# A 2752-byte gap in SBUF ahead of the turned rows of the expert products

## What is computed

```
x = layernorm(x + linear_attention(x))          # 16 heads, five 512x512 weights
x = layernorm(x + cross_attention(x, ctx))      # softmax over 512 positions, 16 heads
x = layernorm(x + experts(x))                   # 16 experts, the best 4 of each token
# the experts, in short:
top_val, top_idx = top_k(x @ router.T + b, 4);  w = softmax(top_val)
gate, up = x @ Wg[e] + bg[e], x @ Wu[e] + bu[e]
gate = min(gate, 7); up = clip(up, -7, 7)
y_e  = ((up + 1) * gate * sigmoid(1.702 * gate)) @ Wd[e] + bd[e]
out  = sum over the 4 experts of w_e * y_e
```

## Time and profile before

| | us |
|---|---|
| median of three runs | 1549.84 |
| runs | 1543.59 to 1550.4 |
| span of the profiled execution, first to last instruction | 1545.7 |
| steady part of the experts, gate of tile 2 to gate of tile 75 | 676.96 |
| one tile of it | 9.27 |

### The profile page before, as it was taken

How to read it: one execution, slowest core, us unless ns; L and a number is a source line. 1 busy time by engine, 2 the same in 40 slices (tenths; PEclk the granted TensorE clock), 3 DMA queues, 4 the chain that set the end, 5 groups by cost and what they waited for, 6 DMA issues and landing times. The chain is left out here.

```text
span 1545.7 us, 27131 instructions
## 1 busy us (share of the span) xinstructions
PE 1438.5 (93%) x7546; PEld 1024.1 (66%) x7546; DVE 953.9 (62%) x1426; ACT 730.2 (47%) x1416; POOL 866.9 (56%) x706
## 2 busy tenths in 40 slices
PE   6999999799999999998959999999999999999990
PEld 5878888434444444443547888888888888888870
DVE  2334343877888778888855555555555555555554
ACT  4212221178787787775433444434344443444233
POOL 4435332555677658644556646656666676476222
PEclk9999999989999999997869999999999999999995
DMA  5201003555485585651175546656666566473336
GB/s 202 85 22 51 14 32 66 84 97 70 88 148 117 89 147 115 92 109 47 56 242 140 152 99 168 169 115 174 153 161 159 156 165 164 118 196 81 64 58 231
DMA packets 93630, 181.36 MB, mean 117 GB/s; under 512 B 19097, under 2 KB 21913, under 8 KB 92473
## 3 DMA queue, kind: packets, MB, share of 16 engines
q1 hardware_dynamic: 73800, 133.04, 34.1%
q0 software_dynamic: 18544, 46.13, 14.9%
q10 hardware_dynamic: 1152, 0.52, 0.2%
HBM read 116.32 MB, written 33.73 MB: 97 GB/s over the span
## 5 line engine op out<-in xcount | busy, mean ns | idle before, releaser
L952 DVE TENSOR_REDUCE stage<-ps_a 128x2 f32<-128x1024 f32 x256 | 300.2, 1218 | 74.5 <-PE ps_a L1301 73.8
L750 ACT ACTIVATE probs<-ps_b 128x512 f32<-128x512 f32 x504 | 274.2, 596 | 52.2 <-PE ps_b L1316 47.7
L2086 POOL TENSOR_TENSOR we_split<-we_raw,we_split 128x512 f32 (+1 forms) x192 | 248.6, 1532 | 84.0 <-ACT we_split L2077 82.1
L2408 PE MATMUL ps_y<-we_split,hT 128*128 x912 | 231.5, 402 | 2.9 <-DVE hT L2330 2.9
L2408 PE MATMUL ps_u<-we_split,xT 128*128 x912 | 230.9, 402 | 0.0
L2408 PE MATMUL ps_g<-we_split,xT 128*128 x912 | 227.0, 397 | 0.5 <-POOL we_split L2086 0.5
L2408 PEld LDWEIGHTS ps_g<-we_split,xT 128*128 128x128 f32 x912 | 172.0, 189 | 42.9 <-issue 0.9
L2408 PEld LDWEIGHTS ps_y<-we_split,hT 128*128 128x128 f32 x912 | 165.5, 188 | 38.1 <-issue 3.3
L2408 PEld LDWEIGHTS ps_u<-we_split,xT 128*128 128x128 f32 x912 | 166.2, 189 | 34.1
L2250 ACT ACTIVATE hT<-ps_h 128x512 fp32r<-128x512 f32 x76 | 45.2, 595 | 303.2 <-PE ps_h L2380 263.4
L2198 POOL DMA_INDIRECT scratch_acc<-x_keep,to_rows x76 | 121.2, 1594 | 109.3 <-issue 49.9
(11 more groups left out here) (345 smaller groups left out, 2208.9 us busy)
## 6 DMA issues: line engine op xcount, KB each, us to landing
we_raw<-in_w_expert SPq DMA_DIRECT2D x180, 256.0 KB
stack<-xT_raw SPq DMA_DIRECT2D x192, 128.0 KB, 5.5
we_bias<-in_b_expert SPq DMA_DIRECT2D x16, 768.0 KB, 4.4
stage<-in_w SPq DMA_DIRECT2D x5, 1024.0 KB, 5.4
xT_raw<-in_xT SPq DMA_DIRECT2D x4, 1024.0 KB, 6.8
x_tok<-in_x POOLq DMA_DIRECT2D x16, 256.0 KB, 3.0
acc_sb<-scratch_acc SPq DMA_DIRECT2D x8, 512.0 KB, 8.0
out<-res_sb SPq DMA_DIRECT2D x8, 512.0 KB, 4.6
```

The lines of the kernel that those rows point to most:

```text
L750: nc.scalar.activation(probs[:, n % 3, h], src[:], ACT.Exp, scale=DH ** -0.5).then_inc(b_kept, 1)
L952: nc.vector.tensor_reduce(out[:, :, i, k % NC], ps_a[i][:], AX.X, ALU.max, negate=True).then_inc(a_kept[i], 1)
L2086: nc.gpsimd.tensor_tensor(lo, W["raw"][:, k, c], hi, ALU.subtract).then_inc(W["lo"], 1)
L2408: mm = nc.tensor.matmul(out[:], left[:, a, c], w[:, bass.ds(par, 1), k, b, c].squeeze(1), start=(n == 0), stop=(n == len(passes) - 1))
```

## The change

One buffer is allocated and never used. It stands between `row_weight` and `xT4`, and has 688 float32 per partition, 2752 bytes. No instruction is added, removed or reordered.

More of the change, by code:

```diff
@@ L2107, in experts @@
         weight = sb("row_weight", [P, U, 2])
+        sb("beside_rows", [P, 688])
         xT = sb("xT4", [P, 2, 2, KC, P], F32R)
```

## The result

With the gap the kernel takes 1537.81 us (median of 6 runs, 1535.17 to 1540.2), against 1549.26 us (median of 6, 1543.59 to 1551.1) for the kernel before. The ratio is 0.9927, with a 95% interval of 0.9911 to 0.9943: 11.4 us or 0.7% faster. The forecast was 1538.8 us.

A forecast was written before the change was run, and what follows sets the result against it. The prediction took TensorE's matmul pace in the experts as the bound: 0.145 us less per tile times 76 tiles is 11.0 us, so 1549.84 - 11.0 = 1538.8 us. The range was 1530 to 1552 us.

The forecast's parts named there:

- The bound: Steady experts: TensorE busy for all of 676.96 us over 73 tiles; time is matmul count times the distance between starts.
- The price of each product: Expert matmuls, priced from like attention runs: gate gains 0.075 us, up and down 0.035 each; 0.145 us per tile.
- The reason: the distance over 512: TensorE's weight load and moving read fall into step when their starts differ by a multiple of 512 bytes: 226.7 against 233 ns.
- Part (2), h: Transposes of h: its distance to ident4 goes from 704 to 2048 bytes; costed at nothing, plus and minus 0.8 us.
- Part (3) and (4): Experts: moved buffers cost ACT and DVE nothing; faster TensorE meets no late weights, some 9 us of cover.
- Rival A: Experts: the longer distance has another cause, so nothing changes; 1549.8 us, chance 0.22.
- Rival B: Experts: all products in step at once, also behind transposes; 0.24 us a tile, 18 us, 1531.6 us; chance 0.09.
- Rival C: Experts: loads starting at the moving operand's residue lose overlap; 0.095 us per tile slower, 7.2 us, 1557; chance 0.07.

The follow-up runs named there:

- hT alone: Against the kernel before, an unused 2752-byte buffer right ahead of hT, so hT starts at 3584 over 4096 as we_split; xT4 and h stay; 1546.66 us, one run.

## Why the prediction was right, and where it was not

**The bound.** Right. TensorE is busy for all of the steady experts before and after, and the gain there, 11.2 us over 73 tiles, is the gain of the kernel, 11.4 us.

**The price of each product.** Right, and in the sum nearly to the number: gate 2.73 us (forecast 2.725), up 2.855 and down 2.829 (2.845 each). The sum per tile was 0.145 us and measured 0.154 (9.273 - 9.120). Two of its terms were off in opposite ways: from the means of before, 2.877 and 2.885, up gained 0.022 us and down 0.055, where 0.035 was taken for each with ends of 0.02 and 0.05. Together they are 0.077 us against 0.070, and that is in part luck, as is the agreement of the totals: 11.0 us were forecast and 11.4 measured, but the interval of the ratio runs from 8.8 to 13.8 us. The attention runs in the like place carried over, even in their settling: behind transposes 2.83 to 2.86 us, without a break 2.72.

**The reason: the distance over 512.** Half right. A distance it is, as the run with moved weights shows, but the period is 256: the 448-byte gap gave the whole gain where I had it out of step. The step that failed is the reading of L1476 against L1416, which left 128 and 0 over 512 and left them over 256 as well; these rows could not tell the two periods apart, and I took the larger. It cost nothing here, since 2752 bytes agree over both. It would have been wrong for half of the gaps that work, those that leave 256 over 512.

**Part (2), h.** The mechanism was missed. I costed the new place of h at nothing, within 0.8 us either way, and looked for it in the transposes. They did not change (0.355 us before and after). Its effect is on the run behind them: with h at 0 over 256, as `ident4` and the weights, up needs 9 matmuls to settle, with h 64 bytes off them at most 6. That is 0.018 us in up and, with gate's end, 0.023 us per tile, 1.7 us over the steady tiles: a loss that the change brings with it against leaving h where it was, outside the bound I gave.

**Part (3) and (4).** Right: no wait came up, the busy times of DVE, ACT and POOL did not move. The cover of the split weights is larger than the 9 us written: in the trace of before the first down on the new expert starts at 1242.08, 15.8 us behind POOL's last piece.

**Rival A**, nothing happens, is out: same instructions, same registers between them, same load on the other engines, and 6.6 ns less per matmul. The Trainium skill, "SBUF — State Buffer", in "Who interferes with whom", has TensorE's two read ports independent and PE waiting on no one. The traces here do not agree with the plain reading of it: with one and the same instruction stream the pace is 226.7, 229.0 or 233.3 ns by where the two operands start. **Rival B**, in step at once, is out for the change: up and down walk through the series. **Rival C**, slower by loads that start with the moving operand, is out: the 2752-byte gap has the distance of exactly 0 (over 4096) once in each product, the 192-byte gap has it at another matmul of the product, and both have the same pace in every matmul of gate.

**What stays open.** That loads and moving reads delay each other is argued from the dependence on their distance; no run took the loads away. Why 192 is a level of its own, and what decides the entry into the settling series, is not explained. Distances below 32 bytes were not tried, nor other shapes.

## What to carry to other kernels

Where TensorE is the bound with a new stationary block for every matmul, compare the start-to-start distance of like matmuls at several places of the trace; if it differs for one shape, compare the SBUF starts of the stationary and the moving operand over 256 bytes. A pad of some tens of bytes can bring them together, and it costs no instruction. This is shown for one shape and type alone, a 128x128 stationary block and 512 moving columns in the type used here; elsewhere it has to be tried. Judge it by the stretch of the timeline that it touches, since the total carries several us from other stages.

## What the runs showed of the hardware that was not expected

- Two operands that agree over 256 bytes: 226.7 ns between matmuls of 512 columns at the 2.4 GHz level; 32 bytes off on either side: 233.3 ns.
- At 192 over 256 the distances repeat as 226, 229, 232 ns; at 64 as 231, 236 or as an even 233.3; at 128 as 238, 229.
- The pace has a memory. With operands that agree over 256, up to 9 matmuls pass behind transposes or behind a run out of step, in one fixed series of distances, before the pace is settled. Where the block that was turned just before stands, relative to `ident4` or the weights, moves the point at which the series is entered (up 2.855 us with h at 0 from them, 2.837 with h at 64), and so does something ahead of the transposes, most likely the run there (hT alone: down enters at 235 or 231, with nothing of its own turning moved).
